# A decoder layer on one core: the feed-forward part permutes the residual instead of its normalised form, and the first steps run in another order

## What is computed

```python
# mixer: in-projection, causal convolution of 4 taps, SSD in chunks of 128, gate, group RMS, out-projection
h = ln(x)
proj = einsum('bsd,od->bso', rms(h) * norm_w, in_proj_w)
x1 = x + h + einsum('bsd,od->bso', y, out_proj_w)
# product with the context, both sides rounded to 0..255
x2 = x1 + matmul(fake_quant(ln(x1)), fake_quant(ctx))
# feed-forward, 16 heads of 32 -> 128 -> 32
t = ln(x2)[:, perm].reshape(b * l, 16, 32)
t = gelu(einsum('bhd,hdm->bhm', t, up), approximate=False)
t = einsum('bhm,hmd->bhd', t, down).reshape(b * l, 512)[:, argsort(perm)]
out = x2 + t
```

## Time and profile before

| | us |
|---|---|
| median of 3 runs (range) | 797.67 (797.21 to 798.57) |
| the profiled execution: its own time | 799.65 |
| its span, first to last instruction | 797.9 |
| PE busy | 769.9 |
| DVE busy | 702.0 |
| POOL busy | 598.2 |
| ACT busy | 553.5 |

### The profile page before, as it was taken

The page is one execution under the profiler, slowest core; times in us unless marked ns, Lnnn a source line. Parts: engine busy times, 40 slices in busy tenths (PEclk is TensorE's granted clock), DMA queues, the critical chain, the costliest instruction groups (busy, mean ns, idle before and its releaser), DMA issues.

```text
span 797.9 us, 14378 instructions
## 1 busy us (share of the span) xinstructions
PE 769.9 (96%) x4180; PEld 605.5 (76%) x4182; DVE 702.0 (88%) x905; ACT 553.5 (69%) x1151; POOL 598.2 (75%) x493
## 2 busy tenths in 40 slices
PE   7988999999999999999999999999999999999976
PEld 6766877787778777787778777787788777887743
DVE  7888999999898989998898988899898989999773
ACT  5676775767766766766766766676767777788574
POOL 6568777787787887788787887788787886787513
PEclk9999999999999999999999999999999999999998
DMA  7552443444434434443435434443334544541004
GB/s 230 178 205 86 153 158 129 142 154 140 152 119 169 158 133 143 145 158 132 147 128 171 158 119 145 157 158 124 144 140 171 171 157 146 186 159 53 0 5 154
DMA packets 44689, 113.21 MB, mean 142 GB/s; under 512 B 5876, under 2 KB 6772, under 8 KB 44660
## 3 DMA queue, kind: packets, MB, share of 16 engines
q1 hardware_dynamic: 44020, 110.76, 40.3%
q0 software_dynamic: 640, 2.10, 0.8%
HBM read 110.35 MB, written 2.49 MB: 141 GB/s over the span
## 4 chain that ended last, share of the span: by engine, by line
PE 86%; DVE 8%; issue 2%; ACT 1%; DMA 1%; POOL 1%; POOLq 0%; SPq 0%; DVEq 0%; ACTq 0%
PE ps_in L1379 17%; PE ps_in L1381 15%; PE ps_in L1380 15%; PE ps_y L1491 8%; PE ps_o L1379 7%; PE ps_o L1381 7%; PE ps_o L1380 7%; PE ps_y L1494 3%; PE ps_t L1453 3%; DVE hid L1082 1%; PE ps_t L1465 1%; DVE e L1138 1%; PE ps_t L1503 1%; DVE stats L1280 1%; DMA res<-in_x 1%
## 5 line engine op out<-in xcount | busy, mean ns | idle before, releaser
L546 POOL TENSOR_TENSOR w_lo<-raw,w_hi 128x512 fp32r<-128x512 f32 x144 | 233.7, 1643 | 104.3 <-ACT w_hi L672 103.0
L1379 PE MATMUL ps_in<-h_hi,w_hi 128*128 128x512 f32 x560 | 226.4, 404 | 2.8 <-DVE gate L1101 2.8
L1381 PE MATMUL ps_in<-h_hi,w_lo 128*128 128x512 f32 x560 | 219.4, 392 | 0.0
L1380 PE MATMUL ps_in<-h_lo,w_hi 128*128 128x512 f32 x560 | 218.4, 390 | 0.0
L727 ACT ACTIVATE e<-e,nag 128x256 f32<-128x256 f32 (+1 forms) x512 | 183.5, 443 | 4.1 <-DVE nag L1152 4.1
L1082 DVE SCALAR_TENSOR_TENSOR hid<-ps_in,curc,hid 128x510 f32<-128x510 f32 x183 | 136.1, 744 | 4.4
L1379 PEld LDWEIGHTS ps_in<-h_hi,w_hi 128*128 128x128 f32 x560 | 105.2, 188 | 33.5 <-issue 9.9
L577 POOL TENSOR_TENSOR e<-e,gm 128x512 f32<-128x512 f32 x64 | 100.2, 1566 | 30.7 <-DVE gm L1126 26.7
L1381 PEld LDWEIGHTS ps_in<-h_hi,w_lo 128*128 128x128 f32 x560 | 105.4, 188 | 23.3
L1380 PEld LDWEIGHTS ps_in<-h_lo,w_hi 128*128 128x128 f32 x560 | 105.5, 188 | 20.5
L692 ACT ACTIVATE hid<-ps_in,curc 128x512 f32<-128x512 f32 x61 | 47.4, 776 | 105.0 <-PE ps_in L1381 104.9
(11 more groups left out here) (235 smaller groups left out, 1205.6 us busy)
## 6 DMA issues: line engine op xcount, KB each, us to landing
e<-acs_rows SPq DMA_DIRECT2D x64, 768.0 KB, 4.5
raw<-in_w_in SPq DMA_DIRECT2D x144, 256.0 KB, 4.7
rawo<-in_w_out SPq DMA_DIRECT2D x64, 256.0 KB, 3.7
craw<-in_ctx SPq DMA_DIRECT2D x8, 256.0 KB, 4.1
res<-in_x SPq DMA_DIRECT2D x4, 256.0 KB, 3.4
x_rows<-raw SPq DMA_DIRECT2D x4, 256.0 KB, 2.3
acs_rows<-z SPq DMA_DIRECT2D x3, 128.0 KB, 2.0
rawo<-in_w_dt SPq DMA_DIRECT2D x1, 256.0 KB, 4.7
```

The source lines that it names most:

```text
L546: pool.tensor_tensor(w_lo[:, slot, :], raw[:, slot, :], w_hi[:, slot, :].bitcast(F32), ALU.subtract).then_inc(s_lo, 1)
L1379: pe.matmul(dst, lh, rh, start=first, stop=False)
L1380: pe.matmul(dst, lh, rl, start=False, stop=False)
L1381: return pe.matmul(dst, ll, rh, start=False, stop=last)
```

## The change

Prologue: after the transposes PE runs the 16 identity matmuls again, into ps_t, ahead of the dt product. In the first four steps, scores come one tile later (after tile 5), and `out_tile(0, 0)` ahead of `turn(0, 2)`. On ACT `conv_tanh` of h 0 goes ahead of `scores_kept`, `gate_tanh(0, 1)` ahead of `exps(0, 1)`, the two taps behind it, and z_high ahead of the next cast and tanh. On DVE `gated(0, 1)` goes ahead of `turned(0, 1)`, `skip_and_gate(0, 0)` ahead of `decays_diagonal(0, 1)`, and `decays_diagonal(0, 2)` moves from step 4 to the end of step 3.

Tail: the row term is ready by halves, and is added before anything is turned. The finished residual x2 is turned, split and permuted, not its normalised form. The norm is applied after that: `spread_terms` multiplies the columns rstd and shift, broadcast along the weights, with the identity, so that each lies as a row over tokens in all partitions; ACT copies the two rows; DVE multiplies and adds them. The ups read that fp32 tile directly, in fp32. The permuted x2 stays in its bank, the downs accumulate onto it (start=False), and DVE only copies the result out. The second turn, the copies, the DRAM round trip and the gather fall away, with the split of up on ACT and POOL. `WARM_B`, matmuls that only occupy PE, goes from 8 to 4 and behind the turns.

```diff
@@ act, first steps
             conv_tanh(0, ("C0", 0))
+            conv_tanh(0, ("h", 0))
             scores_kept()
-            conv_tanh(0, ("h", 0))
             exps(0, 0)
             gate_tanh(0, 0)
+            conv_tanh(0, ("h", 1))
+            gate_tanh(0, 1)
+            exps(0, 1)
             tap0(0, ("h", 2))
-            conv_tanh(0, ("h", 1))
-            exps(0, 1)
-            gate_tanh(0, 1)
+            tap0(0, ("h", 3))
             cast_out(0, 0)
             cast_first(10, 11)
-            tap0(0, ("h", 3))
+            z_high_and_square(0, 0)
             cast_first(11, 12)
             conv_tanh(0, ("h", 2))
-            z_high_and_square(0, 0)
@@ dve, first steps
+            gated(0, 1)
             turned(0, 1)
+            skip_and_gate(0, 0)
             decays_diagonal(0, 1)
-            gated(0, 1)
             taps(0, ("h", 2))
-            skip_and_gate(0, 0)
+            z_low(0, 0)
             conv_silu(0, ("h", 2))
-            z_low(0, 0)
...
             conv_silu(0, ("h", 3))
+            decays_diagonal(0, 2)
             z_low(0, 1)
@@ pe, prologue and first steps
+            for _ in range(WARM):
+                pe.matmul(ps_t[:, 0:P], ident[:, :], ident[:, :], start=True, stop=True)
...
-            project_first(4, 5)
+            project_first(4, 6)
             scores(0)
-            project_first(5, 7)
+            project_first(6, 7)
...
             outputs(0, 1)
+            out_tile(0, 0)
             turn(0, 2)
-            out_tile(0, 0)
@@ act, tail
-            normalise(0)
-            normalise(1)
-            finish_residual(0)
-            finish_residual(1)
-            normalise(2)
-            finish_residual(2)
+            add_row_term(2)
+            add_row_term(3)
+            add_row_term(0)
+            add_row_term(1)
             act.wait_ge(s_ft, 1)
...
+            for k in range(DK):
+                act.activation(f_hi[:, k, :], feature_bank(k), ACT.Copy).then_inc(s_fhi, 1)
+            act.wait_ge(s_sp, 1)
+            act.activation(rstd_row, out_bank(0), ACT.Copy).then_inc(s_spk, 1)
+            act.activation(shift_row, out_bank(1), ACT.Copy).then_inc(s_spk, 1)
@@ dve, tail
             add_product(0)
             add_product(1)
+            row_terms(back)
+            dve.wait_ge(s_px, 2)
+            statistics(0)
+            statistics(1)
             moments(front)
             add_product(2)
+            add_product(3)
+            mean_with_row_term(front)
             norm_terms(front)
...
             for k in range(DK):
                 dve.wait_ge(s_p, k + 1)
-                step_of(dve.tensor_copy(p_hi[:, k, :], feature_bank(k)))
-                dve.tensor_tensor(p_lo[:, k, :], feature_bank(k), p_hi[:, k, :].bitcast(F32), ALU.subtract)\
-                   .then_inc(s_plo, 1)
-            dve.wait_ge(s_xg, 16 * DK)
+                dve.wait_ge(s_spk, 1)
+                step_of(dve.tensor_tensor(e1[:, k, :], feature_bank(k), rstd_row, ALU.mult))
+                dve.wait_ge(s_spk, 2)
+                dve.tensor_tensor(e1[:, k, :], e1[:, k, :], shift_row, ALU.add).then_inc(s_pk2, 1)
             for k in range(DK):
                 dve.wait_ge(s_dn, k + 1)
-                dve.tensor_tensor(x2_rows[k], x2_rows[k], feature_bank(k), ALU.add).then_inc(s_store, 1)
+                dve.tensor_copy(out_rows[k], feature_bank(k)).then_inc(s_store, 1)
@@ pe, tail
+            def spread_terms(two):
+
+                pe.wait_ge(s_lnm, two.start // 2 + 1)
+                for b, term in enumerate((rstd, shift)):
+                    for t in range(two.start, two.stop):
+                        last = pe.matmul(out_bank(b)[:, t * P:(t + 1) * P], term[:, t:t + 1].to_broadcast([P, P]),
+                                         ident[:, :], start=True, stop=True, skip_group_check=True)
+                return last
...
+                for j in heads:
+                    r = slice(FD * j, FD * (j + 1))
+                    last = pe.matmul(ps_o[:, j, :], up_raw[r, k, :], e1[r, k, :], start=True, stop=True,
+                                     skip_group_check=True)
...
             take_part(0, f_hi)
-            turn_residual(3).then_inc(s_xt, 1)
+            take_part(1, f_hi)
+            spread_terms(slice(0, 2))
+            spread_terms(slice(2, 4)).then_inc(s_sp, 1)
             take_part(0, f_lo).then_inc(s_p, 1)
...
+            take_part(1, f_lo).then_inc(s_p, 1)
+            take_part(2, f_hi)
+            pe.wait_ge(s_spk, 2)
+            pe.wait_ge(s_ffw, 32)
             up_pair(0)
             up_pair(1)
```

More of the change, by code:

```diff
@@ L505, in _ @@
             sp.dma_start(raw[:, 1, :], down).then_inc(s_ffw, 16)
-            for k in range(DK):
-                sp.wait_ge(s_xk, k + 1)
-                sp.dma_start(x2_dram[k * P:(k + 1) * P, :], x2_turned[k]).then_inc(s_xs, 16)
             sp.wait_ge(s_out, 16 * DK)
@@ L656, in _ @@
             pool.wait_ge(s_perm, 32)
-            pool.wait_ge(s_xs, 16 * DK)
-            for k in range(DK):
-                pool.indirect_dma_start(x2_rows[k], None, x2_dram[:, :],
-                                        bass.IndirectOffsetOnAxis(ap=perm_col_i[:, k:k + 1], axis=0))\
-                    .then_inc(s_xg, 16)
             for k in range(DK):
@@ L885, in _ @@
             z_high(last_m, CT - 1)
-            act.wait_ge(s_ffw, 32)
-            act.wait_ge(s_in, NIN * GROUPS)
-            act.activation(up_hi, up_raw, ACT.Copy).then_inc(s_uph, 1)
             act.preload_act_table(ACT.Gelu)
@@ L906, in column_sums, with add_row_term @@
                 act.activation(colrow[:, b, :], ps_in[0:1, b, :], ACT.Copy).then_inc(s_cr, 1)
-            def normalise(t):
-                act.wait_ge(s_lnm, t // 2 + 1)
-                act.activation(e1[:, t, :], res[:, t, :], ACT.Identity, scale=rstd[:, t:t + 1],
-                               bias=shift[:, t:t + 1]).then_inc(s_f, 1)
+            def add_row_term(t):
+                act.wait_ge(s_rq, t // 2 + 1)
+                if t < 2:
+                    act.wait_ge(s_px, t + 1)
+                act.activation(x2[t], res[:, t, :], ACT.Identity, bias=rowq[:, t:t + 1]).then_inc(s_late, 1)
             column_sums(0)
@@ L1190, in step @@
                     conv_params(n)
-                decays_diagonal(*lagged(n, t, 2))
+                if not (is_first(n) and t == FIRST_STEPS):
+                    decays_diagonal(*lagged(n, t, 2))
                 gated(*lagged(n, t, 2))
@@ L1275, in _ @@
             mean_square(last_m)
+            one_hot(0)
+            one_hot(1)
             dve.wait_ge(s_r, GROUPS)
@@ L1315, in round_norm, with row_terms, mean_with_row_term, features_low @@
                 dve.tensor_scalar(e1[:, t, :], e1[:, t, :], 255.0, MAGIC, ALU.min, ALU.add).then_inc(s_rn, 1)
+            def row_terms(two):
+                dve.wait_ge(s_q1a, 1 + two.start // 2)
+                dve.tensor_scalar(rowq[:, two], rowsum[:, two], qd[:, 6:7], qd[:, 7:8], ALU.subtract, ALU.mult)\
+                   .then_inc(s_rq, 1)
+            def mean_with_row_term(two):
+                dve.wait_ge(s_rq, 1)
+                step_of(dve.tensor_tensor(mv[:, two, 0], mv[:, two, 0], rowq[:, two], ALU.add))
             def add_product(t):
                 dve.wait_ge(s_pr, t + 1)
+                if t >= 2:
+                    dve.wait_ge(s_late, t - 1)
                 dve.scalar_tensor_tensor(res[:, t, :], out_bank(t), qd[:, 4:5], res[:, t, :],
                                          ALU.mult, ALU.add).then_inc(s_px, 1)
-                dve.wait_ge(s_px, t + 1)
-                statistics(t)
+            def features_low(k):
+                dve.wait_ge(s_fhi, k + 1)
+                dve.tensor_tensor(f_lo[:, k, :], feature_bank(k), f_hi[:, k, :].bitcast(F32), ALU.subtract)\
+                   .then_inc(s_flo, 1)
             front, back = slice(0, 2), slice(2, 4)
@@ L1336, in _ @@
             moments(back)
-            one_hot(0)
+            one_hot(2)
             quant_scales(back)
@@ L1690, in take_part @@
                 return last
-            def take_features(k):
-                take_part(k, f_hi)
-                take_part(k, f_lo).then_inc(s_p, 1)
             def up_pair(i):
                 k, heads = i // 2, (2 * (i % 2), 2 * (i % 2) + 1)
-                pe.wait_ge(s_plo, k + 1)
+                pe.wait_ge(s_pk2, k + 1)
                 wait(pe, s_gl, i - 1)
-                for w, p in ((up_hi, p_hi), (up_hi, p_lo), (up_lo, p_hi)):
-                    for j in heads:
-                        r = slice(FD * j, FD * (j + 1))
-                        last = pe.matmul(ps_o[:, j, :], w[r, k, :], p[r, k, :], start=(w is up_hi and p is p_hi),
-                                         stop=(w is up_lo), skip_group_check=True)
+                for j in heads:
+                    r = slice(FD * j, FD * (j + 1))
+                    last = pe.matmul(ps_o[:, j, :], up_raw[r, k, :], e1[r, k, :], start=True, stop=True,
```

(1 more changed line is left out.)

89 lines of the change are left out of this document (26 added, 63 removed).

## The result

Six executions of the changed kernel have a median of 793.24 us (791.26 to 794.21), against 797.44 (796.74 to 798.57) for six of the kernel before beside them. The ratio is 0.9932, 95% interval 0.9912 to 0.9951, that is 5.4 us faster (3.9 to 7.0); the two medians themselves differ by 4.2 us. The prediction was 790.2 with a range from 787.0 to 793.7: right sign, inside the range near its slow end, and the gain smaller than the 7.5 us of the sum. The profiled execution took 794.21 (span 792.4), against 799.65 (797.9).

The account below looks back on a forecast made before the run. PE, busy 96% of the span, was taken as the bound, so only its waits or slow running could be won. First steps 3.4 plus tail 4.1 make 7.5 us, giving 790.2 us on the runs' median scale; range 787.0 to 793.7.

Parts of the forecast that it names:

- Prologue, 1.7 later: Prologue: the 16 added fp32 matmuls end 1.7 us after the dt product could start, and buy nothing visible.
- First four steps, 2.0: First four steps: `outputs(0, 2)` starts at 60.25 instead of 62.28, 2.0 us earlier, the prologue's cost already paid.
- From 2.0 to 3.4: Behind `outputs(0, 2)`: the clock stays full, 1.7 us more by 67, 3.7 on PE; taken as 3.4 because DVE is close.
- `one_hot` moved: nothing: Tail: the two `one_hot` ahead of the last out-projection's sum fill a DVE wait for POOL and gain nothing.
- Up to the turns: 3.7: Tail: the high part starts at 768.8 instead of 772.50, 3.7 us earlier.
- To the first up: 1.8: Tail: the first up starts at 777.1 instead of 778.92, 1.8 us earlier.
- Ups to the last down: Tail: groups of four ups take 1.0 us; the last down starts 11.6 behind the first up, 2.0 us earlier than before.
- The end: 1.75 behind the last down: End of the tail: last store issued 1.75 us behind the last down (3.9 before), 4.1 us earlier than before.
- The first steps give nothing: Rival, first steps: prologue cost and new waits add up, half clock returns; only the tail gains, 793.6; chance 0.12.
- The tail's rival: Rival, ups: fp32 strips of 32 rows don't overlap, four ups take 3.44 us instead of 1.0; 799.9; chance 0.04.
- Sum: Whole kernel: 3.4 us from the first steps plus 4.1 from the tail, 7.5 us.

Follow-up runs that it names:

- e1: The changed kernel without the second block of 16 identity matmuls in the prologue; no measurement tells its time from the changed kernel's.
- e3: The changed kernel's tail with the prologue and first steps of the kernel before; 3.0 us faster than the kernel before (1.7 to 4.2).
- e7: The kernel before without the stores of the turned residual and their gather; 1.0 us faster than the kernel before (0.1 to 1.8).
- e2: The kernel before with the new prologue and first steps alone, old tail; 1.9 us faster than the kernel before (1.0 to 2.8).
- e9: The changed kernel with down 0 between up pairs 4 and 5, down 1 between 6 and 7; time not to be told from the changed kernel's.
- e10: The changed kernel with gated(0, 2) ahead of z_low(0, 1), take 3 later and split around up pair 4, down 1 behind the last pairs; ratio 0.9955.
- e6: The changed kernel itself, unchanged, measured again beside the kernel before; 4.5 us faster than the kernel before (3.3 to 5.7).
- e12: The changed kernel without the block, gated(0, 2) ahead of z_low(0, 1), and e9's order of ups and downs; 4.8 us faster than the kernel before (3.1 to 6.5).

## Why the prediction was right or wrong

- **Prologue, 1.7 later.** The dt product started at 14.61, as predicted (14.6). At the taps and at the outputs the cost was 1.10, since DVE's small operations, which stood in the way before, no longer did. "Buys nothing" is probably wrong: the half clock over the dt product was seen only without the block, in two of seven, and the mean clocks are higher with it.
- **First four steps, 2.0.** The waits came where the hand-made list had them: none before the scores, none before gate tile 2, 1.53 before `out_tile(0, 0)` (predicted 1.4), 1.61 before `outputs(0, 2)` (1.6). Counted from the transposes these start 1.85 us earlier. The total is right partly by luck: it stands for a gain of 3.7 from the lists less 1.7 for the block, and by e1, which has the lists without the block, these are 2.99 and 1.14, so that two misses nearly cancel. And one reading is wrong: "POOL's own product ends last", so that the sum would stay as it is with DVE at its uncontended rate. In the changed kernel POOL's product ended at 59.41 and DVE's at 60.48, and before, it ran from 59.38 to 61.09 beside DVE's, which ended at 62.18; the split in the earlier trace rows had ended by then. The rule of the Trainium skill (GPSIMD Engine Reference, Key points) did bear on the sum: at the 1.22 us of the earlier trace rows DVE would have ended about 1 us earlier, an estimate.
- **From 2.0 to 3.4: the step that failed.** "No single wait is as long as the 2.8 us one, so the clock stays full and 1.7 us more are won": counted from the transposes 2.42 were won at `outputs(0, 4)`, not 3.7, and only 0.57 of the 1.7. The half clock of the profile before cost 1.6 by this path, and it was won back; but 1.0 was lost again on the same stretch. That loss comes from DVE. `z_low(0, 1)` was not priced; behind the decays it took 1.76 us beside POOL's split and its next product (0.96 at 50.61), and held `gated(0, 2)` at 62.10, just where it was before. Behind `outputs(0, 2)` PE starts gate tile 3 0.8 us later than in e3, and the other 0.3 are small gaps behind it. I had named the rule of the Trainium skill on GpSimd and VectorE contending, and looked only at the decays. The other fault is what the clock was worth. It did stay full, in the profile and nearly always in the changed kernel, but the kernel before has its half clock in one of two places, at one of which it costs nothing, so that 1.7 was the most that could be won and not the mean. The head measured 2.4 in the profile and 1.9 in the medians. The other rule of the Trainium skill named in the prediction (TensorE: Matmul & The Clock Gate, Part 1), by which several short waits could do what a long one did, agrees with the seven profiles that have a stretch at the 1.6 us wait; the other two have the same waits and no stretch.
- **`one_hot` moved: nothing. Up to the turns: 3.7.** The first high part stands 22.96 behind the token sums, before 26.63: 3.67. Right.
- **To the first up: 1.8.** Measured 2.03 by the same count (31.02, before 33.05).
- **Ups to the last down: the second step that was mis-sized.** 11.6 predicted, 12.44 measured (before 11.80). Groups of four ups took 1.14 and 1.28 instead of 1.0, pair 4 came 0.4 later than ACT could take it, and ups 6 and 7 stood behind two downs, for 1.89 us of ACT's time. So the last down came 1.39 earlier, not 2.0.
- **The end: 1.75 behind the last down.** Measured 2.11, the same as in e7, so the last down sets the end, as said. From 3.87 before, that gains 1.76. The tail gave 3.15 instead of 4.1.
- **Rivals.** "The first steps give nothing" did not come true: the head gives 1.9. Its half clock came back in kernels of the same head (e2, e9), and cost 0.5 to 0.6 there. Strips of 32 rows in fp32 overlap: four of them with two passes each took 1.14 us, not 3.44. The tail's rival fell.
- **Sum.** 1.9 to 2.4 and 3.0 to 3.2, instead of 3.4 and 4.1. Both large terms were too large by about 1 us or more, in the same direction; the measured time lies inside the range because the range was wide, half a microsecond from its end. Two divisions are slightly off (3.43 over 15 is 0.229, 3.67 over 8 is 0.46), which changes nothing in the sum.

## What to carry to other kernels

When a chain is laid out by hand, price every instruction on the engine that feeds it, small ones too, at its slow duration wherever the neighbouring engine is busy. A cost that one profile shows (here 1.7 us of half clock) is one of several that its executions have: profile the kernel before more than once before counting on winning it back, and compare starts from a common event, not from the span's start. An order of operations that leaves the bound engine idle is not mended by moving one of them forward; the gelus' waits behind the first pair moved, and their sum was 3.46 us in the changed kernel, 3.00 in e9 and 3.75 in e10.

## What was not expected of the hardware

- A stretch at clock 0.50 (1.2 GHz) came behind waits of PE of 1.6, 1.8, 2.8 and 3.1 us (begins at 60.6 in e9, 13.3 in e7, 48.8 in e3, 63.2 before), and behind the same waits in other executions it didn't come (the changed kernel, e6). Two executions with the same instructions thus differ in whether they have it, and where.
- A DVE copy of 64 columns takes 1.3 us in some executions of the same kernel and 0.2 in others. DVE of the changed kernel and of e6, at the second group's parameters; the first makes PE wait 1.18 us at 126, the second doesn't:

```profile
120.50 1.32 DVE L1119 COPY nag<-naT 128x64 f32 x1
```

```profile
120.21 0.18 DVE L1119 COPY nag<-naT 128x64 f32 x1
```

  This alone sets two executions of one kernel 1.2 us apart. From `outputs(0, 4)` to the token sums these two differ by 2.1 us (658.7 and 656.6) with the same instructions; the rest gathers in steps of under 0.1 us a group. What decides either stays open.
- A group of two up products (two row strips, two fp32 passes each) took 1.13 us in e9 and e12, a group of four 1.14: the second pair was free. The group of two in e9:

```profile
779.63 1.13 PE L1689 MATMUL ps_o<-e,raw 32*128 32x512 f32 x4
```
